# Counting edges in blocks of 32 destinations from four ranges of 8, with masks turned by DMA transposes and rows spread by transposes

## The reference

```
# layer 0: graph convolution
h   = x @ W0
out = segment_sum(h[src] * deg^-1/2[src] * deg^-1/2[dst], dst) + b0     # with self loops
x1  = layernorm(x + out)
# layer 1: 4 attention heads of 256, layer 2: one head of 768; for each:
xl  = x1 @ W
e   = leaky_relu(as[src] + ad[dst]);  e = exp(e - max over dst)
out = segment_sum(xl[src] * e / sum(e), dst) + b
x   = layernorm(out) ... + residual product (x1 @ Wr + br)
```

## Time and profile before

| what | before |
|---|---|
| median of 3 runs | 844.95 us (844.8 to 847.12) |
| the profiled execution's own time | 844.18 us |
| span in its profile | 842.3 us |
| granted TensorE clock, mean | 0.994 |
| PE busy | 808.9 us, 96% |
| DVE busy | 672.1 us, 80% |
| ACT busy | 268.8 us, 32% |
| POOL busy | 60.1 us, 7% |
| counting stage, first L807 to last L807 | 19.21 to 127.70 us |
| x1 stage, first transposes to product of tile 2 | 204.66 to 234.60 us |

### The profile page before, as it was taken

How to read it: one execution, slowest core, us unless ns; L and a number is a source line. 1 busy time by engine, 2 the same in 40 slices (tenths; PEclk the granted TensorE clock), 3 DMA queues, 4 the chain that set the end, 5 groups by cost and what they waited for, 6 DMA issues and landing times.

```text
span 842.3 us, 13750 instructions
## 1 busy us (share of the span) xinstructions
PE 808.9 (96%) x5022; PEld 533.0 (63%) x5022; DVE 672.1 (80%) x1181; ACT 268.8 (32%) x510; POOL 60.1 (7%) x81
## 2 busy tenths in 40 slices
PE   5899998999999999999999998999999999999995
PEld 4577774665554444447888887886666666555553
DVE  7999995777676659999988879969872287996686
ACT  2454456010011201015555455643301107760000
POOL 3000002011103000000000000011110000001111
PEclk9999999999999999999999999999999999999998
DMA  8000004041131353235212104113223342112232
GB/s 306 7 2 2 2 3 170 25 162 57 45 156 70 100 178 124 82 120 201 61 59 86 53 1 138 57 63 126 88 63 94 124 137 76 65 57 75 75 113 71
DMA packets 24588, 73.55 MB, mean 87 GB/s; under 512 B 2756, under 2 KB 3756, under 8 KB 24398
## 3 DMA queue, kind: packets, MB, share of 16 engines
q1 hardware_dynamic: 23262, 67.61, 23.3%
q0 software_dynamic: 1264, 5.11, 1.8%
HBM read 52.40 MB, written 20.31 MB: 86 GB/s over the span
## 4 chain that ended last, share of the span: by engine, by line
PE 89%; DVE 5%; issue 3%; DVEq 2%; ACT 1%; DMA 0%; POOL 0%; SPq 0%; POOLq 0%
PE psum L957 19%; PE psum L984 19%; PE psum L750 18%; PE psum L1065 12%; PE psum L872 8%; PE psum L762 6%; PE psum L814 3%; PE psum L972 1%; PE psum L998 1%; DVEq L1359 1%; PE psum L909 1%; PE psum L937 1%; ACT arena L1072 1%; PE psum L807 1%; PE psum L723 1%
## 5 line engine op out<-in xcount | busy, mean ns | idle before, releaser
L984 PE MATMUL psum<-arena 128*128 128x257 f32 x800 | 175.4, 381 | 2.6 <-DVE arena L1601 1.6
L1072 ACT ACTIVATE arena<-psum 128x160 f16<-128x160 f32 (+6 forms) x188 | 93.4, 528 | 258.9 <-PE psum L750 74.8
L984 PEld LDWEIGHTS psum<-arena 128*128 128x128 f32 x800 | 151.2, 190 | 26.2 <-ACT arena L1072 2.7
L750 PE MATMUL psum<-arena 128*128 128x512 f16 x720 | 159.3, 379 | 2.3 <-DVE arena L1429 1.9
L957 PE MATMUL psum<-arena 128*128 128x512 f16 x960 | 158.5, 326 | 0.2 <-ACT arena L1072 0.2
L957 PEld LDWEIGHTS psum<-arena 128*128 128x128 f16 x960 | 93.5, 97 | 62.3 <-ACT arena L1072 0.5
L750 PEld LDWEIGHTS psum<-arena 128*128 128x128 f16 x720 | 69.3, 98 | 86.4 <-issue 7.0
L1065 PE MATMUL psum<-arena 128*128 128x512 f16 (+2 forms) x600 | 98.4, 326 | 0.0
L1065 PEld LDWEIGHTS psum<-arena 128*128 128x128 f16 x600 | 58.3, 97 | 39.8
L1457 DVE CUSTOM_DVE_ANT_0 arena<-arena 128x1280 bf16<-128x1280 bf16 x50 | 71.0, 1488 | 14.1 <-DMA arena<-as_scratch 8.2
L1175 ACT ACTIVATE arena<-arena 128x640 f32<-128x640 f32 x80 | 64.5, 836 | 49.4 <-DVE arena L1586 49.2
(11 more groups left out here) (173 smaller groups left out, 714.9 us busy)
## 6 DMA issues: line engine op xcount, KB each, us to landing
arena<-in_L_gnn_W_dram SPq DMA_DIRECT2D x22, 384.0 KB, 3.2
r_scratch<-arena SPq DMA_DIRECT2D x10, 512.0 KB, 2.6
arena<-uv_scratch SPq DMA_DIRECT2D x16, 320.0 KB, 4.4
arena<-r_scratch SPq DMA_DIRECT2D x10, 512.0 KB, 3.7
x_scratch<-arena SPq DMA_DIRECT2D x10, 384.0 KB, 4.5
arena<-x_scratch SPq DMA_DIRECT2D x10, 384.0 KB, 3.5
r_scratch<-arena SPq DMA_DIRECT2D x10, 384.0 KB, 2.6
arena<-r_scratch SPq DMA_DIRECT2D x10, 384.0 KB, 3.7
```

The lines of the kernel that those rows point to most:

```text
L750: ins = pe.matmul(o[:, a:b], part[:, k, ds(t * P, P)], w[:, k, a:b], start=(not begun and k == 0 and n == 0 and m == 0), stop=(k == kn - 1 ...
L984: last = pe.matmul(p_att[:, ATT_BANKS[ch][j], 0:HID + 1], pf[n % PSLOTS][:, j * P:(j + 1) * P], xl[ch % H][:, k, 0:HID + 1], start=(k == 0 ...
L1072: act.activation(out_, in_, ACT.Copy, scale=scale).then_inc(signal, 1)
```

## The change

Counting blocks take 32 destinations. Such a block consists of four ranges of 8 destinations; range s uses 4 consecutive edge tiles that begin 2 s tiles behind the block's first one. So a turn has ten edge tiles with a low one-hot table each, shared by the four ranges, and 16 matmuls of 80 columns. The first tile of a block is now chosen so that all four ranges are covered, which changes the prologue's tables and arithmetic. The pieces of `x @ W0` keep their 80 steps, a block in every second step.

C is no longer transposed by PE. SP stores `c_hi` to DRAM after the last block is counted and, once layer 0's product is done, reads it back with ten transposing DMAs into `c_turned`; DVE makes the masks in place from SBUF, after `xl` tiles 2, 3 and 4. `rows_of` uses transposes where it used matmuls with the identity.

```diff
-WD = 16
+WS = 8
+NS = 4
+WD = NS * WS
 NB = NP // WD
+STEPS = 2 * NB
-G = 6
-KSLOTS, CSLOTS = 4, 3
+G = 4
+APART = 2
+GL = (NS - 1) * APART + G
+KSLOTS, CSLOTS = 2, 3
-IOTAS = 8
+IOTAS = 12
+MASKS_AT = {2: range(0, 4), 3: range(4, 7), 4: range(7, T)}
...
-        X1_ORDER = [("tr", 0), ("tr", 1)]
-        X1_ORDER += [s for k in range(KD) for s in [("part", 0, k)] + ([("neg", k - 3)] if k >= 3 else [])] + [("xl", 0)]
-        X1_ORDER += [s for k in range(KD) for s in [("part", 1, k)] + [[("neg", 3)], [("tr", 2)], [("neg", 4), ("tr", 3)], [("neg", 5), ("neg", 6)], [("neg", 7)], [("neg", 8), ("neg", 9)]][k]] + [("xl", 1)]
+        X1_ORDER = [("tr", 0), ("tr", 1)] + [("part", 0, k) for k in range(KD)] + [("tr", 2), ("xl", 0)]
+        X1_ORDER += [("part", 1, k) for k in range(KD)] + [("tr", 3), ("xl", 1)]
...
             sp.wait_ge(S["h_done"], T)
-            weights(1)
+            weights(1, range(3))
+            sp.wait_ge(S["blk_free"], NB)
+            sp.dma_start(c_d, c_hi.rearrange("p t n -> p (t n)")).then_inc(S["c_out"], 16)
+            weights(1, range(3, KD))
...
+            sp.wait_ge(S["c_out"], 16)
+            sp.wait_ge(S["gcn_done"], T)
+            for k in range(T):
+                sp.dma_start_transpose(c_turned[:, :, k * P:(k + 1) * P], c_d[:, k * NP:(k + 1) * NP]).then_inc(S["c_turn"], 16)
...
-                with pe.Fori(0, end):
+                windows = o.rearrange("p (k w) -> p k w", k=T)
+                with pe.Fori(0, end, G):
                     pe.wait_ge(S[f"keys_ready{slot}"], counts[slot])
-                    for i in range(G):
-                        last = pe.matmul(o, ring_lo[slot][:, i // 2, :, i % 2], ring_key[slot][:, i // 2, :, i % 2],
-                                         start=False, stop=False, skip_group_check=True)
+                    for s in range(NS):
+                        for i in range(G):
+                            last = pe.matmul(windows[:, :, s * WS:(s + 1) * WS], ring_lo[slot][:, (s * APART + i) // 2, :, i % 2],
+                                             ring_key[slot][:, i // 2, s * T * WS:(s + 1) * T * WS, i % 2],
+                                             start=False, stop=False, skip_group_check=True)
...
             def rows_of(column, tiles, o):
 
                 for i, t in enumerate(tiles):
-                    last = pe.matmul(o[:, i * P:(i + 1) * P], column[:, t:t + 1].to_broadcast([P, P]), ident, start=True, stop=True)
+                    last = pe.transpose(o[:, i * P:(i + 1) * P], column[:, t:t + 1].to_broadcast([P, P]), ident)
...
-                    dve.tensor_tensor(ring_lo[slot], lo_io.unsqueeze(1).to_broadcast([P, GP, P, 2]), pairs(lo_s, P), ALU.is_equal)
-                    dve.tensor_tensor(ring_key[slot], key_io[b % SUBS].unsqueeze(1).to_broadcast([P, GP, T * WD, 2]),
-                                      pairs(keys, T * WD), ALU.is_equal).then_inc(S[f"keys_ready{slot}"], 1)
+                    dve.tensor_tensor(ring_lo[slot], lo_io.unsqueeze(1).to_broadcast([P, GL // 2, P, 2]), pairs(lo_s, g, GL, P), ALU.is_equal)
+                    for a in range(G // 2):
+                        ins = dve.tensor_tensor(ring_key[slot][:, a].rearrange("p (s n) c -> p s n c", s=NS), key_io[b % SUBS],
+                                                pairs(keys, g + 2 * a, 2 * NS, T * WS), ALU.is_equal)
+                    ins.then_inc(S[f"keys_ready{slot}"], 1)
...
             def mask(t):
 
-                dve.wait_ge(S["neg_tr"], t + 1)
-                dve.tensor_scalar(neg[:, t, :], p_neg[t % 2], 0.0, NEG_BIG, ALU.is_equal, ALU.mult).then_inc(S["neg_ok"], 1)
+                dve.wait_ge(S["c_turn"], 16 * T)
+                dve.tensor_scalar(neg[:, t, :], c_turned[:, t, :], 0.0, NEG_BIG, ALU.is_equal, ALU.mult).then_inc(S["neg_ok"], 1)
...
                 elif what == "xl":
-                    if t == 1:
-                        dve.wait_ge(S["par_b1"], 16)
-                        xl_evict(0)
                     dve.wait_ge(S["xl_done"], t + 1)
                     project(t, H, HID, p_x[t % 2], a_junk)
-                    if t:
-                        xl_evict(t)
+                    if t == 0:
+                        dve.wait_ge(S["par_b1"], 16)
+                        dve.wait_ge(S["c_out"], 16)
+                    xl_evict(t)
+                    for m in MASKS_AT.get(t, ()):
+                        mask(m)
```

More of the change, by code:

```diff
@@ L71 @@
 PAD_DST = 2000
-RANGE_BIG = 1024.0
+RANGE_BIG = 1024
+NO_TILE = RANGE_BIG - LAST_TILE - FRONT
 F16_EXACT = 2048
@@ L261, in gnn_program @@
         x1_sb = x_sb
+        c_turned = at(70 * KB, [T, NP], f16)
         neg = at(70 * KB, [T, NP], bf16)
@@ L710, in _ @@
             pe.wait_ge(S["ranges_f"], 1)
-            for c in range(2):
-                last = pe.matmul(p_rng[:, c * NB:(c + 1) * NB], span[:, c:c + 1], ident[0:NB, 0:NB], start=True, stop=True)
+            for c in range(4):
+                first, some = c % 2 * NB * NS + c // 2 * P, min(P, NB * NS - c // 2 * P)
+                last = pe.matmul(p_rng[:, first:first + some], span[:, c:c + 1], ident[:, 0:some], start=True, stop=True)
             last.then_inc(S["ranges_t"], 1)
@@ L890, in slot_read @@
             def slot_read(t, last):
-                if last and last[0] == "neg":
-                    pe.wait_ge(S["neg_ok"], last[1] + 1)
-                elif last:
+                if last:
                     pe.wait_ge(S["x1t_lo_ok"], last[1] + 3)
@@ L904, in _ @@
                     last.then_inc(S["x1_tr"], 1)
-                    used[t % 2] = (what, t)
-                elif what == "neg":
-                    slot_read(t, used[t % 2])
-                    for k in range(T):
-                        last = pe.transpose(p_neg[t % 2][:, k * P:(k + 1) * P], c_hi[:, k, t * P:(t + 1) * P], ident_h)
-                    last.then_inc(S["neg_tr"], 1)
                     used[t % 2] = (what, t)
@@ L1361, in one_hots, with pairs @@
                 dve.reg_alu(r0, r0, (1 << PACK) - 1, ALU.bitwise_and)
-                first, end = dve.snap(r0, min_val=0, max_val=2 * ETP - G), dve.snap(r1, min_val=G, max_val=2 * ETP)
+                first, end = dve.snap(r0, min_val=0, max_val=2 * EW - GL), dve.snap(r1, min_val=G, max_val=2 * EW)
                 with dve.Fori(first, end, G) as tile:
-                    g = nc.s_assert_within(tile, 0, 2 * ETP - G, skip_runtime_bounds_check_because="the loop ends at 2 ETP at most, in steps of G from its start")
-                    def pairs(v, width):
-                        return v[:, ds(g, G)].rearrange("p (a c) -> p a c", c=2).unsqueeze(2).to_broadcast([P, GP, width, 2])
+                    g = nc.s_assert_within(tile, 0, 2 * EW - GL, skip_runtime_bounds_check_because="the table has GL tiles more than the last start")
+                    def pairs(v, at, tiles, width):
+                        return v[:, ds(at, tiles)].rearrange("p (a c) -> p a c", c=2).unsqueeze(2).to_broadcast([P, tiles // 2, width, 2])
                     dve.wait_ge(S[f"keys_free{slot}"], counts[slot])
-                    dve.tensor_tensor(ring_lo[slot], lo_io.unsqueeze(1).to_broadcast([P, GP, P, 2]), pairs(lo_s, P), ALU.is_equal)
-                    dve.tensor_tensor(ring_key[slot], key_io[b % SUBS].unsqueeze(1).to_broadcast([P, GP, T * WD, 2]),
-                                      pairs(keys, T * WD), ALU.is_equal).then_inc(S[f"keys_ready{slot}"], 1)
+                    dve.tensor_tensor(ring_lo[slot], lo_io.unsqueeze(1).to_broadcast([P, GL // 2, P, 2]), pairs(lo_s, g, GL, P), ALU.is_equal)
[3 more added lines that the diff above has]
+                    ins.then_inc(S[f"keys_ready{slot}"], 1)
                     dve.reg_add(counts[slot], counts[slot], 1)
```

206 lines of the change are left out of this document (101 added, 105 removed).

## The result

The changed kernel takes 826.49 us (median of 4 runs, 825.19 to 827.06) against 846.0 us of the kernel before (median of 4, 844.8 to 847.12). The ratio is 0.9767, 95% interval 0.9745 to 0.979: 2.3% faster, 19.5 us. The prediction was 825: its sum is a step of 19.5 us, taken from a median of 844.95.

A forecast was written before the change was run, and what follows sets the result against it. PE was taken as the bound (89% of the chain), with DVE setting the pace at the start of counting. Terms of +2.0, -11.1, -7.0 and -3.4 make -19.5 us, forecast 825; own range 819 to 831, wider range 817 to 846.

The forecast's parts named there:

- The sum: Whole kernel: prologue +2.0, counting -11.1, x1 stage -7.0, rows by transposes -3.4, together -19.5 us.
- Price of the narrow matmul: Counting on PE: a matmul of 80 columns takes 0.038 us, a block of 32 destinations 0.75 us.
- The step from the one-column row to 80 columns: Counting on PE: 0.025 us at one column shows weights load faster, so 80 columns cost 0.033 plus 0.005 us.
- Counting: Counting stage: 2.7 us gained in the first seven blocks, 7.9 after, 0.5 from waits; 11.1 us, between 8 and 13.
- the extra turn: Last counting block: it needs two turns where the other 39 need one, costing 0.61 us more.
- Prologue: Before counting: PE's first matmul moves to about 7.9, DVE starts 1.5 us later, counting 2.0 us later (0.5 to 3.5).
- the range steps: Prologue, behind PE's first results: twice as many steps with half as many operations in each.
- The x1 stage: From the first product to tile 2's product: 19.5 us against 26.5, 7.0 us gained.
- the new wait: x1 stage: transposes of tile 5 wait for tile 3's buffer, 1.3 us idle; range 0 to 2.
- Transposing DMAs: x1 stage: ten instructions for 3200 KB take 15 to 28 us, with 29 us available and no stall.
- its last safe time: x1 stage: PE stands still if the transposed counts are later than about 241 us.
- 1.6 us of cover: x1 stage: DVE asks for the transposed counts at 239.4, PE stands still only if they come after about 241.

The follow-up runs named there:

- cols40: Changed kernel with the edge matmuls cut to 40 of their 80 columns, same number of weight loads (counts wrong): 819.54 us, one run.
- count_only: Changed kernel with PE's transposes of C, the old x1 order and the rows_of matmuls put back, leaving only the new counting blocks and their prologue: 836.59 us, 0.9896.
- masks_only: Kernel before with only the transposing DMAs and the new order of the x1 stage: 839.55 us, 0.9926.
- rows_only: Kernel before with only rows_of made of transposes instead of matmuls: 841.35 us, 0.9953.
- params_later: Changed kernel with POOL's three broadcast parameter loads issued only after the first three rows of attention values have landed: 824.38 us, 0.9752.
- as_early: Changed kernel with layer 1's attention values made before xl_evict of tile 9, their PE transpose a sixth of a product earlier: 824.47 us, 0.9745.
- identity_first: Changed kernel with POOL making the identity ahead of all iotas: 823.1 us, 0.9732.

## Why the prediction was right, point by point

- **The sum** said -19.5 us and the medians differ by 19.5. The terms were +2.0, -11.1, -7.0, -3.4; with prologue and counting cut at DVE's first table the two traces show +2.3, -11.6, -6.9, -3.4, and +2.5 that had no term. Profile against profile it is 844.18 to 827.06, 17.1 us, 2.4 less than forecast: the missing term but for 0.1. The medians agree with the forecast better than that, since the profiled execution of the changed kernel lies 0.6 us above its median and that of before 1.8 below. That part is luck. The limits that the prediction lists for its terms add up to 821 to 834 and not to the 819 to 831 that it gives as its own range; the measured time lies in both.
- **Price of the narrow matmul**, right to 1 ns. The step from the one-column row to 80 columns held, and cols40 shows why. The Trainium skill's 81 ns for 128 columns ("TensorE: Matmul & The Clock Gate", "Back-to-back issue gap") is not borne out in this kernel: it shows 56 ns at 128 columns and 37 ns at 80.
- **Counting**, right: 11.6 against 11.1. Up to the thirteenth step of before, the seventh block of now, DVE's pace gained 3.4 us (19.25 to 15.88 from its first table) against 2.7 forecast; the rest of the stage fell from 98.6 to 90.4, 8.2 against 8.4. Inside the rest two errors cancel: the block was 0.72 instead of 0.75, and the extra turn was mis-sized, 2.6 us instead of 0.61, by a wait for its own buffer.
- **Prologue**, nearly right in the sum, +2.3 against +2.0, by other parts: PE's first matmul was at 8.54 and not 7.9, DVE took its results 2.3 us later than before (11.51 against 9.20) and not 1.5, and the range steps behind it cost nothing where 0.5 was put. PE's own first block came 3.8 us later in one trace and 2.5 in the other, which costs nothing.
- **The x1 stage**, right: 19.7 against 19.5 forecast, with the new wait of 1.33 against 1.3.
- **Transposing DMAs**, right: 24 us for ten, in the range of 15 to 28. The text's times are in the time line of before. This stage began 9.3 us earlier here (195.39 against 204.66 by the starts of its first matmuls), so DVE was to ask at 239.4 - 9.3 = 230.1 and asked at 230.4. From 202.4 on that left 28 us, as the forecast's own 211.2 to 239.4; 24 were used. (To 241, its last safe time, are 29.8 us, which it calls 29.) Only the 1.6 us of cover that PE was to have behind DVE's question are not there: in the run with twenty transposing DMAs DVE waits 15.4 us and PE loses 15.3. The Trainium skill's "VectorE: DVE Perf Modes", section "The three transpose paths", gives 1309 ns for one tile by itself; 2.4 us for a piece of ten tiles, where ten of these one after the other would be an estimated 13, shows that tiles overlap. The 350 to 400 GB/s of the Trainium skill's "Advanced Engine Details and Errata", section "X-Bar Transpose (TRN2)", were not reached: 3200 KB in 24 us are 137 GB/s.
- **Residual products**, missing. The prediction took the stages behind the change as moved without loss. They had next to no slack: the first trip through DRAM, which nothing in the change touches, varies from 8.3 to 10.7 us, and any execution in which it exceeds about 8.5 us is paid for by PE; in count_only and masks_only it was the second trip that cost 1.3 and 1.9. It can be so in the kernel before, too, since rows_only, which is the same up to there, had a trip of 9.07 us and 0.6 us more than it in this stage.

## What to carry to other kernels

Price a narrow matmul by its columns down to the floor that the trace shows, and check whether a second pass of a loop reuses the buffer that the first still holds. When two engines share a stage, cut it at the start of the one that sets the pace: the other's first instruction can move by a microsecond and cost nothing. When a stretch is shortened, add up the slack of every later stage in which two engines are nearly level, and ask of each small store and reload on such a path which unrelated bulk loads are issued beside it; holding those back cost nothing here, took 2 us away, and left five runs within 0.12 us where the changed kernel's four spread over 1.9. What other engines wait for goes first on POOL: identity ahead of tables was worth 1.4 to 2.4 us in three traces, with runs that spread over 0.8 to 2.0 us. The best version run was the changed kernel with identity first and the values early, 822.5 us.

## What was not expected of the hardware

- A store of 40 KB to DRAM was released after 1.5 us when it was issued by itself or first, and after 3.1 to 4.0 us with POOL's loads of 1.4 MB beside it. A second one took 3.4 to 5.3 us with 768 KB of loads issued on its own queue about a microsecond ahead, and 1.6 to 1.9 with these 3.4 us ahead. DVE's first maximum began 4.5 and 4.8 us after the issue of the three 640 KB broadcasts without POOL's loads (params_later, as_early), and 5.1 (before) and 6.8 us (the changed kernel) after it with them.
- The ten transposing DMAs of 320 KB, 13,000 packets under 512 B by the profile, took 24 us the first time and 19.5 us when nothing else ran beside them.
- Two DVE conversions in the prologue took 0.92 and 1.78 us while POOL made its tables, where the kernel before shows 0.39 and 0.43, and identity_first 0.78 and 0.65. No run isolates what slows them.
